# Layer norms over the feature axis: one centring product, squared and scaled straight out of its PSUM bank

## The chip, the cores and the metric

The kernel runs on one core of one Trainium2 chip. The metric is the device time of one execution in microseconds. The core has a matrix engine (TensorE, PE), a vector engine (VectorE, DVE), an activation engine (ScalarE, ACT), a general engine (GpSimd, POOL) and a queue for transfers (SyncE, SP). Each runs its own list of instructions in order and waits on semaphores where it needs another's result. PSUM is the memory that TensorE writes: here banks of 128 x 512 fp32, named pa, pb, ta, tb, c0, c1 and the double bank sc.

## What is computed

Four layers over 4 batches of 1024 tokens with 128 features, each followed by a layer norm of input plus output:

```python
def _layernorm(x, axis=-1, eps=1e-05):
    m = jnp.mean(x, axis=axis, keepdims=True)
    v = jnp.var(x, axis=axis, keepdims=True)
    return (x - m) / jnp.sqrt(v + eps)
...
x = _layernorm(x + _L0_attn_ref(...))   # linear attention with rotations
x = _layernorm(x + _L0_ffn_ref(...))    # two transformer layers, windows of 64
x = _layernorm(x + _L1_attn_ref(...))   # deformable gather of 33 rows a token
x = _layernorm(x + _L1_ffn_ref(...))    # 8 experts, top-2 gating over tokens
```

Each of the two transformer layers has one more norm in front of its feed-forward, with gain and bias:

```python
h = (h - mu) / jnp.sqrt(var + 1e-05) * lg + lb
h = h @ w1 + b1
```

The change is in the norms of the first two layers only. The last two are normed over tokens in another way and stay.

## The kernel before

Activations lie with features on the 128 partitions and 512 tokens (a half, j = 0 or 1) along the free axis. A mean over features is therefore a product with `meanw`, a 128 x 128 matrix filled with 1/128: every partition of the bank then holds the mean of its token.

A batch has eight such norms, m = 0 to 7. Norms 0 and 1 (halves 0 and 1) follow the linear attention. Norms 2 and 3 stand in front of the feed-forward of the first transformer layer, 4 and 5 in front of the second, and their result `hn` feeds the product with `w1`. Norms 6 and 7 follow the second transformer layer and write `x2`. They run in the order 0, 1, 2, 3, 4, 6, 5, 7 (`NORMS`). Over 4 batches that makes 32 norms.

A norm is two steps, `mean` and `var`, in the program of each engine:

- `mean`: TensorE multiplies `meanw` by the source (L1479). VectorE waits for the bank, subtracts it from the source into `lnc` and gives the bank back (L1118). ScalarE waits for that and squares `lnc` into `lnq` (L839).
- `var`: TensorE multiplies `meanw` by the squares (L1484). ScalarE takes Ln out of the bank (L844) and Exp(-0.5 x) in SBUF (L846). VectorE multiplies `lnc` by the result: for norms 0 and 1 into `x1` (L1123), for 2 to 5 with the gain into `lnc` (L1125), for 6 and 7 into `x2`, a part of `xm` (L1131). For norms 2 to 5 ScalarE then adds the bias and writes `hn` (L849), which the first products of the feed-forward read (L1539).

The banks. The products of projections, norms and feed-forward share pa and pb in turn. The function `plan` goes through TensorE's steps in their order and gives every result the next of the two. A product waits (`wait_free`) until the former user of its bank has been drained. So behind `mean m` in one bank and `var m` in the other, the next result takes the bank of `mean m`: behind norm 0 that is `ao 1`, the output product of the attention's second half (L1466), behind norm 1 the query projection of the first tile (L1491), behind norms 2, 3 and 4 a value projection `v` (L1491), behind norm 5 a product of the feed-forward, behind norm 6 the transposes `x2t 0` of its own result, behind norm 7 the second group of transposes of the next batch (L1372).

The order. The steps have due times in tables (`AT`, `first_times`, `late_times`), and each engine's list is sorted by them once, when the program is built. Batch 0 runs alone. Then a loop of three passes computes batch b in its first part (attention and the two transformer layers) beside the second part of batch b - 1, the gather: GpSimd issues indirect transfers of the rows (L744, three for a chunk, 88 chunks for a batch), VectorE weights a chunk (L1240), TensorE sums its transposes (L1591). A ring of 5 chunk buffers couples them. A tail does the second part of batch 3 and the experts. GpSimd also multiplies the weights of each tile of tokens (L759). On VectorE the weighting of a chunk stands between `mean 7` and `var 7`. On ScalarE, in front of the square of norms 2 and 4, stand the exponentials of the softmax (L881) and two copies (L796).

## Time and profile before

| | us |
|---|---|
| time, median of 3 runs | 2317.84 |
| lowest and highest | 2312.19, 2323.54 |
| the profiled execution, its own time | 2323.0 |
| its span, first to last instruction | 2321.0 |
| TensorE busy | 1669.0 (72%) |
| VectorE busy | 1307.1 (56%) |
| GpSimd busy | 1140.6 (49%) |
| ScalarE busy | 969.2 (42%) |

The mean granted clock of TensorE over the span was 0.853 of full speed. The page lists busy time by engine, and then groups of instructions by their line in the program: how often, how long, and for what the engine waited before. The timeline gives single instructions: start, duration, engine, line, "written<-read" tiles, and in square brackets how long the engine had been idle and whose end released it. A row without brackets had its engine busy until then. Matmuls overlap: the row that follows another on TensorE can begin before its end. An fp32 product of 128 x 512 counts as two instructions.

### The profile page before, as it was taken

What the parts mean: (1) busy time and instruction counts of PE and PEld (TensorE: products, weight loads), DVE (VectorE), ACT (ScalarE), POOL (GpSimd) and SP (SyncE); (2) the same over time, 40 slices, a digit from 0 to 9 for tenths busy, and PEclk for the clock granted to TensorE, in tenths of its full rate; (3) what the DMA queues carried; (4) which work ended last, traced back from release to release, by engine and by line L of the source; (5) the groups of instructions that cost most, each with busy time, mean ns of one, the idle gap of its engine ahead of it and who ended that gap; (6) DMA issues with size and microseconds to landing.
All of it is one profiled execution on the core that took longest, in us unless ns stands there. A gap on an engine that the chain in (4) does not pass through costs nothing.

```text
span 2321.0 us, 34040 instructions
## 1 busy us (share of the span) xinstructions
PE 1669.0 (72%) x11753; PEld 1075.6 (46%) x11753; DVE 1307.1 (56%) x2182; ACT 969.2 (42%) x2341; POOL 1140.6 (49%) x1136
## 2 busy tenths in 40 slices
PE   5667675766687767756878758667777567999967
PEld 3343333434454534435545424355445335766747
DVE  6664643567766734667577436576666344343333
ACT  3355553323445553225444623145455333343431
POOL 0000003467766516477676062776763265777710
PEclk8899997878898978779899978788998778999975
DMA  3000003223333323133333231333333252333311
GB/s 126 10 19 14 14 15 64 64 82 110 114 90 90 94 42 89 50 101 112 98 103 101 42 76 43 101 110 101 101 94 73 46 152 67 103 102 102 102 23 37
DMA packets 92404, 178.45 MB, mean 77 GB/s; under 512 B 21434, under 2 KB 49220, under 8 KB 91972
## 3 DMA queue, kind: packets, MB, share of 16 engines
q0 software_dynamic: 50688, 138.48, 21.4%
q1 hardware_dynamic: 41540, 37.70, 5.8%
q8 instruction: 101, 1.65, 0.3%
q14 instruction: 75, 0.61, 0.1%
HBM read 150.93 MB, written 8.92 MB: 69 GB/s over the span
## 4 chain that ended last, share of the span: by engine, by line
PE 33%; DVE 22%; POOL 15%; issue 14%; ACT 11%; DMA 4%; DVEq 0%; POOLq 0%; SPq 0%; ACTq 0%
POOL pool_c L744 14%; PE c L1591 4%; DVE pool_c L1240 4%; DMA pool_c<-rows_of_x,idx 4%; ACT prob L881 3%; DVE ssq L1144 3%; DVE nmax L1154 2%; PE pb L1491 2%; PE pa L1491 2%; DVE pool_a L1197 2%; PE tb L1372 2%; PE pb L1539 2%; PE pa L1539 2%; PE sc L1656 2%; PE pa L1529 1%
## 5 line engine op out<-in xcount | busy, mean ns | idle before, releaser
L744 POOL DMA_INDIRECT pool_c<-rows_of_x,idx x1056 | 1074.9, 1018 | 1070.7 <-issue 655.9
L1240 DVE TENSOR_TENSOR pool_c<-pool_c 128x768 f32<-128x768 f32 x352 | 341.0, 974 | 307.3 <-DMA pool_c<-rows_of_x,idx 268.5
L1591 PE MATMUL c<-ident,pool_c 128*128 128x128 f32 x2112 | 338.1, 305 | 171.3 <-DVE pool_c L1240 171.1
L1591 PEld LDWEIGHTS c<-ident,pool_c 128*128 128x128 f32 x2112 | 278.8, 158 | 298.9 <-DVE pool_c L1240 211.2
L881 ACT ACTIVATE prob<-sc,nmax 128x128 f32<-128x128 f32 x512 | 180.3, 379 | 126.9 <-DVE nmax L1154 126.8
L796 ACT COPY pool_a<-tb 128x512 f32<-128x512 f32 x188 | 112.1, 596 | 69.6 <-PE tb L1372 69.6
L1491 PE MATMUL pa<-wqkv,pool_a 128*128 128x512 f32 x192 | 115.7, 688 | 16.1 <-DVE pool_a L1197 6.9
L1491 PE MATMUL pb<-wqkv,pool_a 128*128 128x512 f32 x192 | 116.4, 693 | 13.3 <-DVE pool_a L1010 6.4
L1521 PE MATMUL ta<-vmix,pool_a 128*64 128x64 f32 x1024 | 79.0, 236 | 62.0 <-ACT pool_a L796 60.1
L881 ACT ACTIVATION_READ_ACCUMULATOR prob<-sc,nmax 128x1 f32 x512 | 111.4, 218 | 0.0
L1144 DVE TENSOR_REDUCE ssq<-pool_a 128x16 f32<-128x1024 f32 x64 | 77.7, 1214 | 57.8 <-ACT pool_a L857 57.7
L1372 PE MATMUL ta<-ident,pool_a 128*128 128x128 f32 x288 | 54.3, 319 | 75.6 <-DVE pool_a L1167 71.6
L1521 PEld LDWEIGHTS ta<-vmix,pool_a 128*64 128x64 f32 x1024 | 71.1, 149 | 75.2 <-issue 74.8
L1372 PE MATMUL tb<-ident,pool_a 128*128 128x128 f32 x544 | 96.0, 305 | 12.1 <-ACT pool_a L796 10.2
L1372 PEld LDWEIGHTS tb<-ident,pool_a 128*128 128x128 f32 x544 | 70.5, 156 | 61.0 <-issue 51.1
L1539 PE MATMUL pa<-pool_a,w 128*128 128x512 f32 (+1 forms) x96 | 68.1, 800 | 32.6 <-ACT pool_a L849 17.7
L857 ACT ACTIVATE pool_a<-pa 128x512 f32<-128x512 f32 x64 | 38.4, 600 | 117.7 <-PE pa L1491 117.7
L863 ACT ACTIVATE ssq<-ssq 128x16 f32<-128x16 f32 x64 | 13.8, 216 | 175.8 <-DVE ssq L1146 175.8
L1154 DVE TENSOR_REDUCE nmax<-sc 128x8 f32<-128x1024 f32 x64 | 77.9, 1217 | 12.8 <-PE sc L1566 12.8
L1214 DVE TENSOR_TENSOR pool_a<-pool_a 128x1024 f32<-128x1024 f32 x64 | 80.4, 1256 | 5.9
L1206 DVE TENSOR_TENSOR pool_a<-pool_a,rot 128x512 f32<-128x512 f32 x128 | 82.7, 687 | 0.1
L1372 PEld LDWEIGHTS ta<-ident,pool_a 128*128 128x128 f32 x288 | 37.0, 161 | 95.5 <-DVE pool_a L1167 84.1
(404 smaller groups left out, 3354.9 us busy)
## 6 DMA issues: line engine op xcount, KB each, us to landing
pool_c<-rows_of_x,idx POOLq DMA_INDIRECT x1056
vmix<-vring SPq DMA_DIRECT2D x128, 128.0 KB
rows_of_x<-x2tok SPq DMA_DIRECT2D x16, 256.0 KB
xtok<-in_x SPq DMA_DIRECT2D x4, 512.0 KB, 4.4
x_of_all<-x2tok SPq DMA_DIRECT2D x8, 256.0 KB, 2.4
out<-pool_c SPq DMA_DIRECT2D x8, 256.0 KB, 2.6
wqkv<-in_wqkv SPq DMA_DIRECT2D x1, 1536.0 KB
xtok<-x_of_all SPq DMA_DIRECT2D x3, 512.0 KB, 6.3
```

The costliest lines, as they stand in the source:

```text
L744: pool.indirect_dma_start(gat[:, n % GB, s, :], None, table, bass.IndirectOffsetOnAxis(ap=idx[:, t, SC * c + s:SC * c + s + 1], axis=0),). ...
L796: nc.scalar.copy(dst, src[:, :] if view is None else view(src)).then_inc(empty(key), 1)
L881: ins = nc.scalar.activation(prob[:, n % 2, pr, e, :], sc[:, e, P * pr:P * (pr + 1)], ACT.Exp, bias=nmax[:, n % 2, e, pr:pr + 1], accum_ou ...
L1144: V.tensor_reduce(ssq[:, t % 2, 0, :], sq[:, :, :].rearrange("p w (h d) -> p (w h) d", h=HB), AXX, ALU.add).then_inc(SEM["b_ss"], 1)
L1154: V.tensor_reduce(nmax[:, n % 2], sc[:, :, :].rearrange("p e (r k) -> p e r k", r=PAIRS), AXX, ALU.max, negate=True).then_inc(SEM["b_max"], 1)
L1206: V.tensor_tensor(r2[:, :, :, at:at + 32], qn[:, :, :, o:o + 32], ap3(rot[:, l, t, 1, 0, at:], [[DH, 2], [0, HB], [1, 32]]), ALU.mult).the ...
L1240: V.tensor_tensor(g4, g4, wv, ALU.mult).then_inc(SEM["c_prod"], 1)
L1372: ins = PE.transpose(out[:, P * i:P * (i + 1)], src(i), ident[:])
L1491: mm(out[:, :], hT[:, P * n:P * (n + 1)], wqkv[:, l, c:c + INNER], start=True, stop=True).then_inc(full(key), 1)
L1521: ins = mm(out[q, DH * (2 * pr + e):DH * (2 * pr + e + 1)], PT[:, n % 2, pr, e, q], v[:, 2 * pr + e, :], start=True, stop=True, skip_group ...
L1539: mm(out[0:w, :], w1[:, l, c:c + w], hn[:, :], start=True, stop=True).then_inc(full(key), 1)
L1591: ins = mm(out[:, c:c + P], x, ident[:], start=(i == 0 and k == 0), stop=(i == BCH - 1 and k == len(parts) - 1), is_transpose=True, skip_g ...
```

## The change

`centre` is a new matrix, the identity less 1/128, made on VectorE once at the start (one instruction of 128 x 128). The first product of a norm uses it in place of `meanw`, so that the bank holds source minus mean. VectorE's subtraction (L1118) is gone. ScalarE squares out of the bank into `lnq`, VectorE scales out of the bank in step `var`, and only that gives the bank back. The semaphore `ln_out` is gone: who waited for it waits for the bank to be drained. The tables of due times and the plan of banks are the same, so every result keeps its bank and its turn.

```diff
+            V.tensor_scalar(centre[:], ident[:], 1.0 / D, None, ALU.subtract)
...
                 elif what == "mean":
                     m, = a
-                    wait_drained(act, ("mean", m), b)
-                    nc.scalar.activation(lnq[:, m % 2, :], lnc[:, m % 2, :], ACT.Square).then_inc(SEM["ln_square"], 1)
+                    src = wait_filled(act, ("mean", m), b)
+                    nc.scalar.activation(lnq[:, m % 2, :], src[:, :], ACT.Square).then_inc(SEM["ln_square"], 1)
...
                     if 2 <= m < 6:
-                        wait(act, "ln_out", b, nth(m) + 1)
+                        wait_drained(act, ("mean", m), b)
...
-                        wait(dve, "f_shift", b, 2 * (m - 2) + 2 + (m == 5))
-                        src = h2[:, :]
-                    elif m >= 6:
-                        wait(dve, "f_res", b, m - 5)
-                    mean = wait_filled(dve, ("mean", m), b)
-                    V.tensor_tensor(lnc[:, m % 2, :], src, mean[:, :], ALU.subtract).then_inc(empty(("mean", m)), 1)
                 elif what == "var":
                     m, = a
                     wait(dve, "ln_rstd", b, nth(m) + 1)
+                    mean = wait_filled(dve, ("mean", m), b)
                     if m < 2:
-                        V.tensor_tensor(block_of(x1, m), lnc[:, m % 2, :], lnq[:, m % 2, :], ALU.mult).then_inc(SEM["ln_out"], 1)
+                        V.tensor_tensor(block_of(x1, m), mean[:, :], lnq[:, m % 2, :], ALU.mult).then_inc(empty(("mean", m)), 1)
                     elif m < 6:
-                        V.scalar_tensor_tensor(lnc[:, m % 2, :], lnc[:, m % 2, :], col(LG + m // 2 - 1), lnq[:, m % 2, :], ALU.mult, ALU.mult).then_inc(SEM["ln_out"], 1)
+                        V.scalar_tensor_tensor(lnc[:, m % 2, :], mean[:, :], col(LG + m // 2 - 1), lnq[:, m % 2, :], ALU.mult, ALU.mult).then_inc(empty(("mean", m)), 1)
...
-                        V.tensor_tensor(x2[:, BLK * (m - 6):BLK * (m - 5)], lnc[:, m % 2, :], lnq[:, m % 2, :], ALU.mult).then_inc(SEM["ln_out"], 1)
+                        V.tensor_tensor(x2[:, BLK * (m - 6):BLK * (m - 5)], mean[:, :], lnq[:, m % 2, :], ALU.mult).then_inc(empty(("mean", m)), 1)
...
-                    mm(out[:, :], meanw[:], src, start=True, stop=True).then_inc(full(("mean", m)), 1)
+                    mm(out[:, :], centre[:], src, start=True, stop=True).then_inc(full(("mean", m)), 1)
...
-                    wait(pe, "ln_out", b, nth(6 + j) + 1)
+                    wait_drained(pe, ("mean", 6 + j), b)
```

On VectorE, in the opening of batch 0, the list holds before the change (`pb` in the second row is the bank of `mean 0`, in the fifth that of `ao 1`, the output product of the attention):

```order
50 L1118 TENSOR_TENSOR lnc<-x,pb 128x512
51 L1084 TENSOR_TENSOR lnc<-sc,lnq 128x512
52 L1090 TENSOR_TENSOR lnc<-lnc,xtok 128x512
53 L1123 TENSOR_TENSOR x<-lnc,lnq 128x512
54 L1094 SCALAR_TENSOR_TENSOR x<-pb,cols,xb 128x512
55 L1118 TENSOR_TENSOR lnc<-x,pa 128x512
```

and after it:

```order
51 L1086 TENSOR_TENSOR lnc<-sc,lnq 128x512
52 L1092 TENSOR_TENSOR lnc<-lnc,xtok 128x512
53 L1119 TENSOR_TENSOR x<-pb,lnq 128x512
54 L1096 SCALAR_TENSOR_TENSOR x<-pb,cols,xb 128x512
55 L1011 COPY pool_a<-x 64x512
```

The subtractions are gone and nothing else changed places: the scaling (53 in both) now reads pb, and the row behind it reads what TensorE writes into the same pb afterwards.

On TensorE, at norm 2 of batch 0, the rows after the change are these (before it they are the same but for `meanw` in the first): `centre` is the first product of the norm, the next is the second, then come the value projection, the transposes `oT`, and the first two products of the feed-forward.

```order
254 L1475 MATMUL pb<-pool_a,centre 128x512
255 L1480 MATMUL pa<-lnq,meanw 128x512
256 L1487 MATMUL pb<-wqkv,pool_a 128x512
257 L1368 MATMUL tb<-ident,pool_a 128x128 x4
258 L1535 MATMUL pa<-pool_a,w 128x512
259 L1535 MATMUL pb<-pool_a,w 128x512
```

Row 256 takes the bank of row 254: nothing moved, but its wait for pb is now a wait for the scaling and no longer for the subtraction.

## Rows read from the trace of the kernel before

**Rows 1.** The page, part 4: chain of work that ended last, share by engine.

```profile
PE 33%; DVE 22%; POOL 15%; issue 14%; ACT 11%; DMA 4%; DVEq 0%; POOLq 0%; SPq 0%; ACTq 0%
```

**Rows 2.** Groups by line: ScalarE's squares, count, busy time and mean ns, idle before them.

```profile
L839 ACT ACTIVATE lnq<-lnc 128x512 f32<-128x512 f32 x32 | 20.4, 639 | 88.1 <-DVE lnc L1118 88.0
```

**Rows 3.** Timeline, batch 0, norms 0 and 1: start us, us, engine, line.

```profile
70.50 0.63 ACT L835 ACTIVATE lnq<-lnq 128x512 f32<-128x512 f32 x1
70.96 0.69 DVE L1118 TENSOR_TENSOR lnc<-x,pb 128x512 f32<-128x512 f32 x1 [1.28 <-PE pb L1479]
...
73.32 1.02 PE L1466 MATMUL pb<-lnc,ow 128*128 128x512 f32 x2
...
74.91 0.69 DVE L1123 TENSOR_TENSOR x<-lnc,lnq 128x512 f32<-128x512 f32 x1 [1.93 <-ACT lnq L846]
...
76.41 1.10 PE L1479 MATMUL pa<-x,meanw 128*128 128x512 f32 x2 [2.06 <-DVE x L1094]
...
79.91 1.02 PE L1491 MATMUL pa<-wqkv,pool_a 128*128 128x512 f32 x2
...
81.49 0.69 DVE L1123 TENSOR_TENSOR x<-lnc,lnq 128x512 f32<-128x512 f32 x1 [2.48 <-ACT lnq L846]
...
83.12 1.22 DVE L1144 TENSOR_REDUCE ssq<-pool_a 128x16 f32<-128x1024 f32 x1
```

**Rows 4.** Timeline, batch 0, norm 2: ScalarE, TensorE and the next bank.

```profile
174.78 0.70 ACT L839 ACTIVATE lnq<-lnc 128x512 f32<-128x512 f32 x1
...
175.53 1.13 PE L1484 MATMUL pa<-lnq,meanw 128*128 128x512 f32 x2 [1.99 <-ACT lnq L839]
...
176.49 1.02 PE L1491 MATMUL pb<-wqkv,pool_a 128*128 128x512 f32 x2
...
178.86 0.72 ACT L849 ACTIVATE pool_a<-lnc,cols 128x512 f32<-128x512 f32 x1 [0.82 <-DVE lnc L1125]
...
180.56 1.28 ACT L901 ACT_TABLE_LOAD   x1
```

**Rows 5.** Timeline, batch 0, norm 4: its second product.

```profile
322.24 2.07 PE L1484 MATMUL pa<-lnq,meanw 128*128 128x512 f32 x2 [1.99 <-ACT lnq L839]
```

**Rows 6.** Timeline, batch 2, norms 0 and 1, while GpSimd gathers.

```profile
966.07 1.12 PE L1466 MATMUL pb<-lnc,ow 128*128 128x512 f32 x2 [0.58 <-DVE lnc L1090]
...
968.27 0.69 DVE L1123 TENSOR_TENSOR x<-lnc,lnq 128x512 f32<-128x512 f32 x1
...
971.64 0.96 DVE L1240 TENSOR_TENSOR pool_c<-pool_c 128x768 f32<-128x768 f32 x1 [2.02 <-DMA pool_c<-rows_of_x,idx]
...
981.28 1.91 PE L1491 MATMUL pa<-wqkv,pool_a 128*128 128x512 f32 x2
```

**Rows 7.** Timeline, batch 2, norm 2: the projection behind the norm, and the scaling.

```profile
1128.84 1.92 PE L1491 MATMUL pb<-wqkv,pool_a 128*128 128x512 f32 x2
1129.19 0.75 DVE L1125 SCALAR_TENSOR_TENSOR lnc<-lnc,cols,lnq 128x512 f32<-128x512 f32 x1 [4.28 <-ACT lnq L846]
```

**Rows 8.** Timeline, end of batch 2's pass, norm 7.

```profile
1379.68 1.02 PE L1479 MATMUL pb<-xb,meanw 128*128 128x512 f32 x2
...
1386.98 0.96 DVE L1240 TENSOR_TENSOR pool_c<-pool_c 128x768 f32<-128x768 f32 x1 [2.29 <-DMA pool_c<-rows_of_x,idx]
1387.34 2.77 PE L1591 MATMUL c<-ident,pool_c 128*128 128x128 f32 x12
...
1388.97 2.01 DVE L1131 TENSOR_TENSOR xm<-lnc,lnq 128x512 f32<-128x512 f32 x1 [1.02 <-ACT lnq L846]
```

**Rows 9.** Timeline, batch 1, norm 2 beside GpSimd's own multiply.

```profile
636.11 0.69 DVE L1118 TENSOR_TENSOR lnc<-pool_a,pb 128x512 f32<-128x512 f32 x1 [1.29 <-PE pb L1479]
636.21 1.54 POOL L759 TENSOR_TENSOR pool_c<-pool_c 128x264 f32<-128x264 f32 x2
```

**Rows 10.** Timeline, batch 3, norm 7 and the transposes that wait for it.

```profile
1877.09 1.96 DVE L1131 TENSOR_TENSOR xm<-lnc,lnq 128x512 f32<-128x512 f32 x1 [1.14 <-ACT lnq L846]
...
1879.10 0.66 PE L1372 MATMUL c<-ident,xm 128*128 128x128 f32 x4 [0.87 <-DVE xm L1131]
```

More of the change, by code:

```diff
@@ L354, in build @@
         meanw = sb("meanw", [P, P])
+        centre = sb("centre", [P, P])
         blockd = sb("blockd", [P, D // G])
@@ L505, in build @@
             "x_loaded": 16, "a_rot": 8, "a_scan": 16, "a_state": 2, "a_zero": 1, "a_att": 1, "a_square": 2, "a_rstd": 2, "a_y": 3,
-            "ln_square": 8, "ln_rstd": 8, "ln_out": 8,
+            "ln_square": 8, "ln_rstd": 8,
             "b_shift": 8, "b_square": 32, "b_ss": 32, "b_rn": 32, "b_cos": 16, "b_sin": 32, "b_qk": 16,
@@ L1096, in first @@
                     m, = a
-                    src = block_of(x1 if m < 2 else xb, m % 2)
                     if 2 <= m < 6:
@@ L1134, in first @@
                     if l == 0:
-                        wait(dve, "ln_out", b, j + 1)
+                        wait_drained(dve, ("mean", j), b)
                     else:
```

## The prediction

> **What bounds the kernel now.** I read first the chain of work that ended last, then the groups by line for the lines that the change touches, and then the timeline around each of the eight norms, in batch 0 and in the passes of the loop, since each has another limit. The chain has no one engine [rows 1]: TensorE 33%, VectorE 22%, GpSimd 15%, ScalarE 11%. The kernel is bound by hand-overs between engines, and a shorter step helps only where that step was the last to arrive. ScalarE's 32 squares waited 88.0 us in all for the subtraction in front of them [rows 2]. That number tempts: a subtraction of 0.69 us with its hand-over is 0.7 us, and 32 of them are 22.4 us. But idle time before a square is not time lost, and the same edit makes the next user of the bank wait for the end of the norm. Both have to be read place by place.
>
> **Batch 0, norms 0 and 1: slower.** Nothing runs beside batch 0. Its first norm [rows 3]: the subtraction begins at 70.96. Without it the square has to wait for ScalarE's own Exp (70.50 + 0.63 = 71.1) and not for 70.96 + 0.69 = 71.65, so the norm is 0.5 us earlier; its scaling begins at 74.4 and not at 74.91, and ends at 75.1. The output product `ao 1` goes into the bank of norm 0. It began at 73.32, under the norm, since the subtraction had given the bank back. Now it begins at 75.1, takes the 1.1 us of a lone product, and VectorE reads it at 76.2 and not at 74.91 + 0.69 = 75.6. Norm 1 thus starts about 0.6 us later than its 76.41. It then saves a whole subtraction (0.7) and scales at 81.4, practically the old 81.49, until 82.1. The query projection, which takes its bank, began at 79.91 and now begins at 82.15; the pair ends two products later (2 x 1.0) at 84.2, the square of the second is 0.6, and the reduction that waits for it begins at 84.8 and not at 83.12: **+1.7 us**.
>
> **Batch 0, norms 2 to 4: slower.** The square of norm 2 at 174.78 has no bracket [rows 4]: ScalarE came to it from its own work, and the subtraction was hidden. No gain. The value projection takes the norm's bank: at 176.49 before, now not before the scaling is over, just ahead of ScalarE's bias step at 178.86. It ends at 180.0, the transposes behind it at 180.5, and ScalarE's two copies (0.5 each: between 178.86 + 0.72 and 180.56 there are two) end at 181.5, where the table for the Gelu is loaded; before that was 180.56: **+1.0 us**. Norm 4 has the same order: **+1.0 us**. Norm 3 has only one copy behind the projection, and two transposes on TensorE stand ahead of its second product. Between nothing and norm 2's 1.0 I take the middle: **+0.5 us**. Norms 5 and 6 come to ScalarE behind its own work too, and their bank goes to someone who needs the result of the norm anyway: 0. Batch 0 together: 1.7 + 1.0 + 0.5 + 1.0 = **+4.2 us**. Making `centre` is one small instruction of VectorE in its first chain: +0.1.
>
> **The passes of the loop, norms 0 and 1: nothing.** There GpSimd's gather sets the pace: VectorE waits for rows to land [rows 6], 2.02 us before the weighting at 971.64. The output product began at 966.07; now it waits for the scaling at 968.27 to end (968.96), ends at 970.1, and VectorE has read it by 970.9, still 0.7 us before the rows land. The scaling itself stands behind the weighting of a chunk, so it is not earlier either. If that cover were gone, each opening would cost 0.6 us as in batch 0. The query projection at 981.28 came after the scaling of norm 1 already. Queued behind the output product on TensorE are sums of chunks; they free buffers of a ring of five, and are late by some 2 us where GpSimd needs them several chunks on.
>
> **The passes, norms 2 to 4: nothing, with a spread.** Here the square did wait for the subtraction. The value projection began at 1128.84 and the scaling at 1129.19 [rows 7]. Without the subtraction the scaling is at 1128.5 and ends at 1129.2, so the projection is 0.4 us later and what hangs on the scaling 0.7 earlier. ScalarE needs both in turn. I take 0 for each of the 9 places. The ends are a whole subtraction gained (-0.7) and the 1.0 lost of batch 0, together -6.3 to +9.
>
> **Norm 7: faster.** Its first product had run at 1379.68 [rows 8], but the subtraction stood on VectorE behind the weighting of a chunk that landed late, and square, second product and the sums behind it followed. Now ScalarE squares at once, and the second product is done before the next weighting (1386.98 + 0.96 = 1387.94). The pass ends on TensorE with the sums of that chunk: the last half of the pair that took 2.77 from 1387.34 to 1390.11, so 1387.95 + 1.4 = 1389.3, or 1388.8 at the faster rate. I take -1.0 at the end of batches 1 and 2: **-2.0 us**. The end of batch 0 lies under GpSimd's gathers: 0. In batch 3 the transposes of x2 wait for the scaling [rows 10]: it began at 1877.09, 1.14 after the weighting ahead of it, and took 1.96. Now it begins at 1875.95. TensorE has one chunk's sums to do first (0.9 to 1.4), so the transposes start near 1877.1 and not at 1879.10: **-2.0 us**.
>
> **How long the scaling takes.** Beside GpSimd's multiply, the scaling of norm 7, both inputs in SBUF, took 2.01 and 1.96 us [rows 8, 10]; the subtraction of norm 2, one input in PSUM, took 0.69 us with that multiply started 0.1 us after it [rows 9]. I use 0.7 us for the scaling out of the bank in all places. The Trainium skill, "SBUF — State Buffer", section "Who interferes with whom", says that a VectorE instruction with two SBUF inputs contends with a GpSimd instruction that reads SBUF, and one with at most one SBUF input does not. By it four scalings would be 1.3 us shorter; the sum is the same without it, since the new scaling begins ahead of the multiply.
>
> **The clock.** Norm 2's second product followed a pause of 1.99 us and took 1.13 [rows 4]; norm 4's followed the same pause and took 2.07 [rows 5]. So products run at either of two levels after equal pauses, and one product at the lower level costs 0.94. The held bank stretches five pauses of TensorE in batch 0 beyond 2 us, and the missing subtraction shortens others. I take one product at the lower level more, rounded to +0.7. The Trainium skill, "TensorE: Matmul & The Clock Gate", section "HAM oscillation — how this bites in real kernels", describes a kernel whose waits let the clock drop again and again. It speaks against a change that makes TensorE wait for a bank, and is rival C.
>
> **The sum.** 4.2 + 0.1 - 2.0 - 2.0 + 0.7 = +1.0 us. The profiled execution was 2323.0 us with a span of 2321.0, so 2324.0; against the median of 2317.84 the same sum gives **2318.8 us**. TensorE, VectorE and ScalarE are less busy or the same, and no transfer changes.
>
> **Rivals.**
> A, faster: the 88.0 us were mostly on the chain. Then each of 32 norms is 0.7 us shorter and the longer hold is hidden: 2317.8 - 22.4 = 2295.4. For it: the squares did wait, and VectorE loses 32 instructions. Against it: rows 3, 4 and 6, where the next user of the bank, ScalarE's own work or a landing comes last. It decides if over half of the squares outside batch 0 are on the chain.
> B, slower: the held bank costs in every batch what it costs in batch 0, and norm 7 gives nothing: 4 x 4.2 = 16.8, 2334.6. Its place is the projection behind norms 0 to 4; it decides where the 0.7 us of cover before the landing [rows 6] and the 0.7 of the scaling [rows 7] are used up.
> C, slower by the clock: all five held products of all four batches run at the lower level: 20 x 0.94 = 18.8, 2336.6. Against it: in the passes chunk sums stand between.
>
> **How the numbers follow.** Forecast 0.68, A 0.17, B 0.10, C 0.05. The forecast's own spread is -6.3 to +9 around 2318.8, thus 2312 to 2328, and the runs shown scatter by 5 us either way. The range 2307 to 2332 takes that in and some of the partial forms of A and B, and leaves about 2 in 10 out. Within 0.5% (11.6 us) is about what a measurement of this kernel can tell from no change. Faster by more is A in its fuller forms, 0.18 with the edge of the forecast; slower is B and C, 0.15; the same is 0.67.
>
> **What would show it.** In batch 0 the reduction behind norm 1 at 84.8 (before 83.12) and the table load behind norm 2 about 2.7 us after its old time; the first gather of GpSimd some 4 us later. In the passes the output product of norm 0 directly behind the scaling, with VectorE still waiting for the landing after it. At norm 7 the square more than 3 us earlier and the scaling 0.7 us long directly behind the weighting. The forecast is wrong if the first gather is not later, or if the length of the second and third pass changes by more than 3 us.

## The result: slower by 13 us, outside the forecast

| | us |
|---|---|
| before, median of 6 runs (lowest, highest) | 2321.6 (2312.2, 2323.9) |
| after, median of 6 runs (lowest, highest) | 2334.7 (2331.6, 2340.6) |
| after / before | 1.0064, 95% interval 1.0043 to 1.0086 |
| profiled execution after: span | 2333.1 (before 2321.0) |
| forecast | 2318.8, range 2307 to 2332 |

The change costs 13.1 us by medians and 14.9 by means (0.64%; the interval of 0.43% to 0.86% is 10 to 20 us). TensorE's instructions are the same but for the matrix in the first product of a norm, yet the page gives it 1680.2 us busy where it gave 1669.0; VectorE has 26.7 us less. The chain has moved from VectorE and GpSimd to TensorE [rows 1] (the page, part 4, after):

```profile
PE 36%; DVE 21%; issue 13%; POOL 13%; ACT 12%; DMA 4%; DVEq 0%; POOLq 0%; SPq 0%; ACTq 0%
```

ScalarE's wait ahead of the squares, the tempting 88.0 us [rows 2], is now a wait for the product, and did not vanish: 33.6 us for one bank here and 28.3 us for the other, together 61.9.

```profile
L840 ACT ACTIVATE lnq<-pb 128x512 f32<-128x512 f32 x16 | 9.7, 605 | 33.6 <-PE pb L1475 33.6
```

**Where the time went.** The first product of norm 0 in batch 0 starts 1.1 us earlier than before, and GpSimd's first gather 15.2 us later (393.29, was 378.12). From there to the end of the span the two profiles differ by 3.1 us in favour of the changed kernel. The windows view of TensorE, from each first product of a norm to the next (norms 0, 1, 2, 3, 4, 6, then the first gather; columns: window, its length, TensorE busy, instructions, granted clock, DMA share, GB/s). Before:

```profile
69.82:76.41 6.59, 3.08 (x7) 1.00 0.00 0
76.41:172.41 96.00, 62.83 (x532) 0.93 0.08 17
172.41:236.40 63.99, 42.32 (x302) 0.89 0.06 13
236.40:319.12 82.72, 58.42 (x494) 0.96 0.08 17
319.12:352.20 33.08, 25.43 (x191) 0.85 0.07 16
352.20:378.12 25.92, 16.15 (x80) 0.90 0.15 41
```

After:

```profile
68.73:76.39 7.66, 3.71 (x6) 0.88 0.00 0
76.39:177.12 100.73, 66.91 (x532) 0.86 0.07 17
177.12:245.68 68.56, 45.67 (x302) 0.85 0.06 12
245.68:331.03 85.35, 61.32 (x495) 0.92 0.07 16
331.03:367.51 36.48, 27.66 (x190) 0.77 0.07 15
367.51:393.29 25.78, 17.00 (x80) 0.84 0.15 42
```

The same products (a few records differ in number): 308.3 us long with 208.2 busy before, 324.6 with 222.3 after. 14.0 of the 16.3 us are TensorE being busy longer, and the granted clock has fallen in every stretch.

**What happens at a held product.** A product is called held here when it has to wait for the scaling because its bank is kept until then. Batch 0, norms 0 and 1, after (timeline; answers to rows 3):

```profile
73.12 0.69 DVE L1119 TENSOR_TENSOR x<-pb,lnq 128x512 f32<-128x512 f32 x1 [1.56 <-ACT lnq L847]
73.96 1.49 PE L1462 MATMUL pb<-lnc,ow 128*128 128x512 f32 x2 [2.26 <-DVE x L1119]
...
76.39 2.04 PE L1475 MATMUL pa<-x,centre 128*128 128x512 f32 x2 [0.94 <-DVE x L1096]
...
79.12 2.07 PE L1480 MATMUL pb<-lnq,meanw 128*128 128x512 f32 x2 [0.69 <-ACT lnq L840]
...
83.45 2.04 PE L1487 MATMUL pa<-wqkv,pool_a 128*128 128x512 f32 x2 [2.26 <-DVE x L1119]
...
85.28 1.91 PE L1487 MATMUL pb<-wqkv,pool_a 128*128 128x512 f32 x2
...
87.87 1.22 DVE L1140 TENSOR_REDUCE ssq<-pool_a 128x16 f32<-128x1024 f32 x1 [3.66 <-ACT pool_a L858]
```

`ao 1` stands directly behind the scaling, as forecast. But in front of it TensorE was idle for 2.26 us, where before the product had filled this time, and what follows runs at the lower of its two levels (1.2 instead of 2.4 GHz): not one product, but nearly all work to 87 us. The granted clock over 74.0 to 87.2 us is 0.52; before it was 1.00 over the same work (69.8 to 83.1 us). From norm 0's first product to the reduction it was 13.30 us before and is 19.14. Norm 2 (answers to rows 4) shows the same, down to the transposes:

```profile
180.21 1.97 PE L1480 MATMUL pa<-lnq,meanw 128*128 128x512 f32 x2 [1.96 <-ACT lnq L840]
...
184.38 0.72 ACT L850 ACTIVATE pool_a<-lnc,cols 128x512 f32<-128x512 f32 x1 [0.82 <-DVE lnc L1121]
184.50 2.05 PE L1487 MATMUL pb<-wqkv,pool_a 128*128 128x512 f32 x2 [2.32 <-DVE lnc L1121]
...
186.34 1.06 PE L1368 MATMUL tb<-ident,pool_a 128*128 128x128 f32 x4
...
187.19 1.92 PE L1535 MATMUL pa<-pool_a,w 128*128 128x512 f32 x2
...
188.58 1.28 ACT L902 ACT_TABLE_LOAD   x1
```

Norm 4 (rows 5) likewise: its value projection took 2.04 us after a pause of 2.32.

### The profile page after: what moved, and what is told of

Its sections match the earlier page's. It is cut to its first block, busy times and chain, and to the rows that moved or that the text cites. A ratio compares the mean times of both kernels' runs of the same rounds, so it can differ in the third digit from the quotient of the medians.

```text
span 2333.1 us, 33988 instructions
## 1 busy us (share of the span) xinstructions
PE 1680.2 (72%) x11745; PEld 1081.7 (46%) x11753; DVE 1280.4 (55%) x2151; ACT 970.2 (42%) x2341; POOL 1137.4 (49%) x1136
## 4 chain that ended last, share of the span: by engine, by line
PE 36%; DVE 21%; issue 13%; POOL 13%; ACT 12%; DMA 4%; DVEq 0%; POOLq 0%; SPq 0%; ACTq 0%
POOL pool_c L745 12%; PE c L1587 4%; DMA pool_c<-rows_of_x,idx 3%; DVE pool_c L1236 3%; PE pa L1487 3%; ACT prob L882 3%; DVE ssq L1140 3%; PE pb L1487 2%; DVE nmax L1150 2%; PE tb L1368 2%; PE pb L1535 2%; DVE pool_a L1193 2%; PE pa L1535 2%; PE sc L1652 1%; PE ta L1368 1%
## 5 line engine op out<-in xcount | busy, mean ns | idle before, releaser
L1487 PE MATMUL pa<-wqkv,pool_a 128*128 128x512 f32 x192 | 121.6, 720 | 23.3 <-DVE lnc L1121 7.0
L1487 PE MATMUL pb<-wqkv,pool_a 128*128 128x512 f32 x192 | 118.6, 704 | 27.1 <-DVE lnc L1121 11.5
L1368 PE MATMUL tb<-ident,pool_a 128*128 128x128 f32 x544 | 99.0, 312 | 12.1 <-ACT pool_a L797 10.2
L1205 DVE TENSOR_TENSOR pool_a<-pool_a,rot 128x1024 f32<-128x1024 f32 x64 | 83.3, 1301 | 2.2
```

The costliest lines, as they stand in the source:

```text
L1205: V.tensor_tensor(qn, qn, ap3(rot[:, l, t, 0, 0, :], [[DH, 2], [0, HB], [1, DH]]), ALU.mult).then_inc(SEM["b_cos"], 1)
L1368: ins = PE.transpose(out[:, P * i:P * (i + 1)], src(i), ident[:])
L1487: mm(out[:, :], hT[:, P * n:P * (n + 1)], wqkv[:, l, c:c + INNER], start=True, stop=True).then_inc(full(key), 1)
```

## The experiments

Theory H: the longer hold is the cause, and most of its price is the clock of the products behind the stretched pause. Its rivals: D, something else in the change; the hold's waits alone, without the clock. On the place there are two theories: B0, the loss arises in batch 0; PA, it arises in the passes. On the pause there are two: S, the pause of the hold is what matters; E, the pause ahead of the norm's second product counts alike.

Each row of the table is one profile. Lengths of batch 0 in the profiles, in us (a norm 2, 3 or 4 is measured from its first product to ScalarE's table load):

| kernel | norm 0 to reduction | norms 2, 3, 4 | norm 0 to first gather |
|---|---|---|---|
| before | 13.3 | 8.2, 8.1, 9.1 | 308.3 |
| before_again | 15.2 | 8.9, 8.1, 9.1 | 312.2 |
| changed (after) | 19.1 | 11.5, 9.3, 11.6 | 324.6 |
| after_again | 18.9 | 10.6, 9.5, 10.8 | 318.6 |
| hold_alone | 20.7 | 10.6, 9.7, 11.3 | 322.7 |
| wait_in_batch0 | 20.6 | 10.6, 9.7, 11.4 | 323.7 |
| wait_in_batch0b | 20.2 | 11.5, 9.7, 11.3 | 323.1 |
| fill_hold_only | 15.2 | 10.2, 9.5, 9.3 | 315.3 |
| fill_square_only | 18.9 | 10.6, 11.7, 10.6 | 321.6 |
| fill_pauses | 15.3 | 9.3, 11.7, 9.2 | 317.4 |
| old_and_fill | 15.1 | 8.5, 9.1, 8.5 | 313.4 |
| turn_bank | 11.9 | 7.8, 9.5, 8.5 | 313.2 |
| turn_but_norm3 | 11.8 | 7.8, 9.1, 7.8 | 311.9 |

Seven more profiles (late_norms_new, the four runs of the wait in the passes, the two of new_in_passes) have the old norms 0 to 4 in batch 0, and took 311.6 to 315.3. With before and before_again the nine give a mean of 313.1; the five that hold and fill nothing (changed, after_again, hold_alone, wait_in_batch0, wait_in_batch0b) give 322.5, and their lowest, 318.6, lies above the highest of the nine. So the first profile of before was the luckiest of nine, and the hold costs 9.4 us in batch 0, not the 16.3 that one pair of profiles shows.

**hold_alone: the hold without the rest.** The old norm, but the subtraction signals by a semaphore of its own, and the scaling gives the bank back. Against the kernel before it comes down to this:

```diff
-V.tensor_tensor(lnc[:, m % 2, :], src, mean[:, :], ALU.subtract).then_inc(empty(("mean", m)), 1)
+V.tensor_tensor(lnc[:, m % 2, :], src, mean[:, :], ALU.subtract).then_inc(SEM["ln_sub"], 1)
...
-... lnq[:, m % 2, :], ALU.mult).then_inc(SEM["ln_out"], 1)
+... lnq[:, m % 2, :], ALU.mult).then_inc(empty(("mean", m)), 1)
```

> The old norm (mean by meanw, subtraction on VectorE into lnc, square and scaling from lnc), with one difference: the bank of the mean is given back only by the scaling, as in the changed kernel. So only the longer hold is left of the change. Theory H (the longer hold is the cause: the projection behind a norm waits for the scaling, and the stretched pause of TensorE is followed by products at the lower clock): batch 0 is as late as in the changed kernel or later, first gather of GpSimd near 393 to 396 us where before had 378.1, and the whole near 2335 to 2342. Theory D (the cause lies in what else changed: the squares and scalings out of PSUM, or the missing work of VectorE, which shifts when everything behind starts): first gather near 378 to 381, the whole within 4 us of before, 2318 to 2326.

Measured: 1.0077 (1.0048 to 1.0105), median 2339.7 beside 2322.2. (Here and below: time by that of the kernel before, measured beside it, with the 95% interval.) First gather 392.3. The hold alone costs as much as the change or more; D falls.

**turn_bank: the change without most of the hold.**

```diff
-    "mean": lambda m: [(("mean", m), PROJ)],
+    "mean": lambda m: [(("mean", m), TURN if m in (0, 1, 2, 4) else PROJ)],
```

> The changed kernel, but the centring products of norms 0, 1, 2 and 4 go into the banks ta and tb, which the transposes use, so that the next product finds pa or pb free while the norm runs. The subtraction stays away, the hold hurts nobody but the transposes. Theory H: batch 0 gets back what it lost but for norm 3, and gains the missing subtraction at norms 0 and 1 (0.5 + 0.7): first gather 376 to 381, the whole 2312 to 2322. If the hold cost only its waits and the clock fell for another reason, the first gather stays at 388 or later and the whole at 2330 or more. Theory A (a subtraction that is on the chain nearly everywhere, hidden so far by the hold): 2298 to 2306.

Measured: 1.0000 (0.9977 to 1.0022), first gather 383.3. The loss is gone, as H says. The first gather is 2 us behind the 376 to 381 that H named; that range had been reckoned from the 378.1 of the first profile. Rival A falls too: with the hold nearly gone, 32 missing subtractions give nothing that can be measured in the whole. They do show in place, 11.9 us at norms 0 and 1 where the nine old profiles have 13.3 to 15.2. Norm 3, still held, takes 9.5 where they have 8.1 to 9.1.

**fill_pauses: the hold with a busy TensorE.** In batch 0, products of `ident` by `ident` are added, into banks that are overwritten next: five in the pause ahead of a norm's second product, eight in the pause of the hold. Norm 3 has only the first five.

```diff
-                    wait(pe, "ln_square", b, nth(m) + 1)
                     out = wait_free(pe, ("var", m), b)
+                    if at_start(b):
+                        for _ in range(5):
+                            mm(out[:, 0:P], ident[:], ident[:], start=True, stop=True)
+                    wait(pe, "ln_square", b, nth(m) + 1)
                     mm(out[:, :], meanw[:], lnq[:, m % 2, :], start=True, stop=True).then_inc(full(("var", m)), 1)
+                    nxt = {0: ("qT", 0, 0), 1: ("qT", 0, 0), 2: ("oT", 0, 4), 3: None, 4: ("oT", 1, 4)}.get(m)
+                    if at_start(b) and nxt is not None:
+                        out = wait_free(pe, nxt, b)
+                        for _ in range(8):
+                            mm(out[:, 0:P], ident[:], ident[:], start=True, stop=True)
```

> The changed kernel with products added in batch 0 alone, whose results are overwritten before anything reads them: 5 of 128x128 ahead of each second product of a norm, while TensorE waits for the square, and 8 behind it, into the bank of a transpose that comes next, while it waits for the held bank. Waits and hold stay as in the changed kernel, only TensorE is no longer idle in them. If most of the 15 us that batch 0 lost are products at the lower clock (theory H with the clock as its larger part: 13.2 us more busy time for the same products): granted clock of 70 to 180 us back to 0.93 or more, first gather 380 to 386, the whole 2320 to 2328. If the waits themselves are the 15 us: first gather at 393 or later, the whole 2334 to 2340.

Measured: 1.0012 (0.9990 to 1.0034), median 2326.6; 1.0064 without the fill. The norms 0 and 1 take 15.3 us instead of 19.1 with the same waits, norm 2 9.25 instead of 11.46. The granted clock of 70 to 180 us is 0.91, where 0.93 or more was expected. At norm 3 the added products came in the way of the norm's own second product, which starts 5.7 us behind the first instead of 3.3 (11.7).

**late_norms_new: the change only where nobody is held** (norms 5, 6, 7; 0 to 4 in the old form).

> The new form only for norms 5, 6 and 7, whose bank nobody waits for who doesn't need the norm's result anyway; norms 0 to 4 in the old form. Theory H: no product is held, batch 0 as before (first gather 378 to 379), and norm 7 gives what the prediction said, 1 us in two passes and 2 at the end of the third: 2315 to 2320, 2 to 5 us below before. If norm 7's gain is taken back by the next wait, 2320 to 2323. Theory D: slower than before in part, 2325 or more.

Measured: 0.9992 (0.9971 to 1.0013), median 2320.8. No loss; the gain of 2 to 5 us isn't shown. Its first gather came at 384.3, where 378 to 379 was expected, with norms 0 to 4 that are those of before. So one profile of the old form doesn't tell the length of batch 0.

**Long passes.** Beside every run from here to new_in_passes, the kernel before itself took 2531 to 2566 us and not 2322. Batch 0 is as long as elsewhere. The passes are not: in the profiles of before and before_again, from norm 0 of one batch to that of the next, the second pass took 484 and 548 us, the third 488 and 561, and the rest behind it 872 and 967. That is more than the 30 us for a pass that some of the expectations below name. Of these runs only the ratios, each against the kernel before beside it, and the lengths of batch 0 are used. The chain of before_again has an entry that the page of before lacks:

```profile
PE 33%; DVE 19%; issue 16%; another core or an unknown queue 11%; ACT 10%; POOL 9%; DMA 2%; DVEq 0%; SPq 0%; POOLq 0%; ACTq 0%
```

All twelve profiles with long passes have this entry, and none of the eight others. In before_again GpSimd waits 54 times, 108.6 us in all, between its gathers for what the profile puts down to another core or an unknown queue. What that is stays open.

**wait_in_batch0, wait_in_passes: the hold as a bare wait.** Before, with one wait added on TensorE:

```diff
             reach(eng, drained[bank], (b + (bank in CB)) * turns[bank] + n)
+            if n:
+                last = next((k for k, v in where.items() if v == (bank, n - 1)), None)
+                if last and last[0] == "mean" and last[1] in (0, 1, 2, 3, 4) and at_start(b):
+                    wait(eng, "ln_out", b, nth(last[1]) + 1)
             return psum[bank]
```

`last` is the former user of the bank. In wait_in_passes and its repeats the condition ends in `not at_start(b)`.

> The kernel before with one thing added, in batch 0 alone: the product that takes the bank of norms 0 to 4 (ao 1, a query projection, three value projections) also waits for the scaling of that norm. No instruction is added, left out or moved. Theory B0 (the loss arises in batch 0, where nothing else fills TensorE, and is carried to the end): first gather of GpSimd 8 to 15 us later than in the kernel before, the whole 2330 to 2338. Theory PA (the 12 to 15 us of batch 0 in one profile were mostly the clock's scatter, and the loss is made in the passes): first gather within 5 us, the whole 2320 to 2327.

Measured: 1.0044 (1.0017 to 1.0071), 7.8 us more by medians and 11.7 by means. First gather 392.2, where before_again has 381.5. Not an instruction differs from before but that wait. Norm 2 there:

```profile
185.17 2.05 PE L1495 MATMUL pb<-wqkv,pool_a 128*128 128x512 f32 x2 [2.32 <-DVE lnc L1129]
```

> The same added wait, but in the three passes of the loop and not in batch 0. Theory B0: chunk sums and landings cover it, as the prediction held: the whole 2319 to 2326. Theory PA: the whole 2330 to 2338, and the passes together 8 to 15 us longer than in the kernel before. Between the two, a share of the loss in each: 2326 to 2330 here and about as much there.

Measured: 0.9999 (0.9967 to 1.0032). With long passes the wait cost nothing there.

> The kernel before, with the products of the run fill_pauses added in the same places of batch 0 (5 of 128x128 ahead of the second product of a norm, 8 behind it, overwritten before anything reads them). It is the control of that run, which was 8 us below the changed kernel. If filled pauses help because the hold had stretched them, they do little here: 2319 to 2324. If they help in any kernel, since the clock of batch 0 is held up: 2312 to 2318, and then only the difference between this run and fill_pauses is the price of the hold itself.

Measured: 1.0006 (0.9979 to 1.0034), batch 0 of 313.4 us, the mean of the old form. Filled pauses are no gain of their own; what fill_pauses gave back was the hold's. The 4.0 us between this batch 0 and that of fill_pauses are the hold with its pauses filled.

> The kernel before, unchanged, to see how far one profiled execution of it stands from another, stage by stage. If the length of batch 0 is the same in each execution, the first gather is at 378 and every norm within 1 us of the first profile; if TensorE's clock makes it scatter, as the run late_norms_new suggests (its norms 0 to 4 are those of before, and its first gather came at 384.3), it lies anywhere between 376 and 386, and the length of the whole stays in 2313 to 2331.

Measured: 1.0011 (0.9973 to 1.0048), batch 0 3.9 us longer than in the first profile: TensorE's clock scatters. Norm 2's second product took 1.13 us in the one and 1.89 in the other after pauses of 1.99 and 1.98.

**fill_hold_only, fill_square_only: which pause it is.** The two halves of fill_pauses.

> The changed kernel with only half of the added products of fill_pauses: 8 of 128x128 behind the second product of a norm in batch 0, in the pause that the held bank makes, none ahead of it. Theory S (the pause that the hold stretches to 2.3 us is what lets the clock fall; the pause before the second product was there before and matters little): nearly as good as both fills, first gather 386 to 388 where the changed kernel had 393.3, the whole 5 to 8 us below the changed kernel. Theory E (both pauses count alike): first gather 389 to 391, the whole about 4 us below it.

> The changed kernel with the other half: 5 products of 128x128 ahead of each second product of a norm in batch 0, in the pause in which TensorE waits for the square, none behind it. Theory S: the clock still falls in the hold, first gather 390 to 393, the whole 0 to 3 us below the changed kernel. Theory E: as the other half, first gather 389 to 391, about 4 us below.

Measured against before: 1.0068 (1.0037 to 1.0100) and 1.0096 (1.0063 to 1.0130); batch 0 315.3 and 321.6 us, first gather 383.9 and 390.5. The products of the hold's pause give back 7.2 us on the mean of the five held profiles, those of the square's pause 0.9, or some 3 if the 2.4 us by which they delay norm 3's second product are added. So batch 0 speaks for theory S. The wholes don't: the changed kernel was not measured beside them, and both stand above the kernel before with intervals that overlap. The loss of fill_hold_only in the whole must lie mostly behind batch 0, in the long passes. In fill_hold_only, norms 0 and 1 (timeline):

```profile
71.43 1.95 PE L1521 MATMUL ta<-ident 128*128 128x128 f32 x16
...
73.86 1.10 PE L1495 MATMUL pb<-lnc,ow 128*128 128x512 f32 x2 [0.47 <-DVE x L1152]
...
81.12 1.10 PE L1528 MATMUL pa<-wqkv,pool_a 128*128 128x512 f32 x2 [0.48 <-DVE x L1152]
...
83.74 1.22 DVE L1173 TENSOR_REDUCE ssq<-pool_a 128x16 f32<-128x1024 f32 x1 [1.86 <-ACT pool_a L877]
```

The products wait for the scaling as in the changed kernel, but run 1.10 us and not 1.49 and 2.04.

> Again the added wait of norms 0 to 4 in the three passes and not in batch 0, since in the call of wait_in_passes the passes of every kernel were some 30 us longer than usual, with rows landing later, and a wait is covered more easily there. If the cover is there at the usual length too, the whole is within 3 us of the kernel before; if it was only the late rows that covered it, 5 to 12 us above.

Measured: 1.0069 (1.0040 to 1.0097), where the same kernel had 0.9999. Not settled by these two.

> As turn_bank, but norm 3, whose projection was still held there, in the old form: no product is held anywhere, and all other norms go without the subtraction. In turn_bank the stages behind norms 0, 1, 2 and 4 of batch 0 were 0.7 to 1.7 us shorter than with the old form and that behind norm 3 2.3 to 5 us longer. If stages add up: first gather 376 to 380, the whole 2 to 6 us below the kernel before. If the passes take nothing from the missing subtraction and the clock eats the rest: within 2 us of it.

Measured: 1.0042 (1.0012 to 1.0072), both expectations missed. Batch 0 is 311.9 us, 1.2 less than in turn_bank, and the first gather came at 382.5 instead of 376 to 380; the whole is slower where it should be faster. With the long passes even the form that holds nothing lost 10 us, and this stays unexplained.

> The changed kernel itself, beside the other three of this call, to see how firm its batch 0 is from one execution to the next. Theory B0: first gather again at 391 to 394 and the whole 10 to 15 us above the kernel before. If the first profile showed an unlucky clock: first gather at 386 or less, the whole 0 to 7 us above.

Measured: 1.0108 (1.0076 to 1.0139), +24 us by medians; batch 0 at 318.6 us, 6 less than in the first profile and still above all old ones. The first gather, 387.4, lies between the two expectations: part of the 324.6 of the first profile was an unlucky clock.

> Again the kernel before with the wait for the scaling added in batch 0 alone, hoped for on a chip where the passes have their usual length. Theory B0: first gather near 392, the whole 10 to 13 us above the kernel before, as much as the changed kernel or 2 us less. Theory PA: 3 to 6 us above.

Measured: 1.0047 (1.0021 to 1.0073), +8.1 us by medians, between the two theories; the first gather, 391.7, is where B0 put it.

> Again the wait in the passes alone, whose two runs before contradict each other (0 and 15 us above the kernel before, both with passes 30 us longer than usual). Theory B0: 0 to 3 us above the kernel before where the passes have their usual length. Theory PA: 7 to 12 us above.

Measured: 1.0051 (1.0029 to 1.0072), +11.6 us by medians, as PA says.

> The changed form in the passes and the old form for norms 0 to 4 of batch 0, where nothing covers the held bank. Theory B0: no loss in batch 0 (first gather 378 to 384), and the gain at norm 7 that the prediction held is all that is left: 2 to 5 us below the kernel before. If the passes give nothing from the missing subtraction: within 2 us of it. Theory PA: 5 to 10 us above.

```diff
+        def form(m, b):
+            return "old" if m in OUTN and at_start(b) else "new"
```

`OUTN` is (0, 1, 2, 3, 4). Measured: 1.0080 (1.0052 to 1.0107), +22 us by medians: more than either theory named. With long passes most of the loss lies in them.

The two runs that follow had passes of the usual length (before: 2325.7 us).

> The wait in the passes alone, once more. Three calls gave 0, +15 and +12 us beside the kernel before, all with passes about 30 us longer than in the kernel's usual runs. If this call has passes of usual length: Theory B0 says 0 to 3 us above the kernel before, Theory PA 7 to 12 us. If its passes are long again, only the mean of four such calls follows, and the question stays open for the usual length.

Measured: 1.0032 (1.0016 to 1.0048), +5.6 us by medians and +7.6 by means: between the two theories.

> Old form for norms 0 to 4 in batch 0, changed form in the passes, once more. At passes of usual length: Theory B0 says 2 to 5 us below the kernel before; if hold and missing subtraction cancel in the passes, within 2 us; Theory PA 5 to 10 us above. With long passes it was 20 us above.

Measured: 1.0007 (0.9989 to 1.0024), 1.6 us less by medians. So in passes of the usual length the held bank costs about 7 us (hold_alone, 16.4 us by means with 9.6 of them in batch 0, says the same), and the missing subtraction gives back about as much, give or take 4.

The profiles say so less clearly. From first product to table load, the nine norms 2 to 4 in the passes sum to these, at the usual length:

| form in the passes | us |
|---|---|
| old (before, late_norms_new) | 79.9, 80.6 |
| old and held (hold_alone, wait_in_passes4) | 89.7, 87.9 |
| changed (after, fill_pauses, new_in_passes2) | 84.2, 89.4, 79.7 |

How a gain can come about shows at norm 2 of batch 2. Before (the first row is the norm's second product; rows 7 have the next ones):

```profile
1125.70 2.07 PE L1484 MATMUL pa<-lnq,meanw 128*128 128x512 f32 x2 [1.51 <-ACT lnq L839]
```

wait_in_passes4:

```profile
1136.98 2.07 PE L1488 MATMUL pa<-lnq,meanw 128*128 128x512 f32 x2 [1.52 <-ACT lnq L843]
...
1141.37 2.04 PE L1495 MATMUL pb<-wqkv,pool_a 128*128 128x512 f32 x2 [1.04 <-DVE lnc L1129]
```

new_in_passes2:

```profile
1128.03 1.12 PE L1516 MATMUL pa<-lnq,meanw 128*128 128x512 f32 x2 [0.76 <-ACT lnq L862]
...
1131.48 1.13 PE L1523 MATMUL pb<-wqkv,pool_a 128*128 128x512 f32 x2 [1.67 <-DVE lnc L1157]
```

Without the subtraction the pause ahead of the second product is 0.76 and not 1.51 us, and both products ran at the upper level. It need not be so: norm 2 of the three batches took 8.1 us each time in new_in_passes2, and 11.0, 11.1 and 8.1 in the changed kernel, which has the same form there.

## Why the prediction was wrong, point by point

- **The 88.0 us are not on the chain:** right. turn_bank lacks all 32 subtractions and holds hardly anything, and stands at 1.0000. Rival A is out.
- **Norms 0 and 1 of batch 0, +1.7:** the place, the order and the wait were right, the size was not. The reduction was to start at 84.8 and started at 87.9. The mean of the two profiles of the changed kernel is 19.0 us, that of the nine old ones 14.4: +4.7. With the hold's pause filled it is 15.2, which is +0.8.
- **Norms 2, 3 and 4, +1.0, +0.5, +1.0:** by the same means +2.1, +1.1 and +2.1. Again the wait was right and what follows it missing.
- **The waits together, +4.2:** near in sum, and not place by place. With all pauses filled, the hold costs 4.0 us in batch 0 (fill_pauses beside old_and_fill), but of its norms 0 and 1 have 0.2, norms 2 and 4 have 0.7 each and norm 3 has 2.6. That the sums agree is partly luck.
- **The clock, +0.7: the step that failed.** It priced one product more at the lower level. The rows used for it (norm 2 and norm 4 after equal pauses of 1.99) told that such a pause may or may not cost; they said nothing of one that is 2.3 us long and comes soon after another. In the five profiles that hold and fill nothing the value projection behind norms 2, 3 and 4 took 2.04 or 2.05 us in 14 of 15 cases (1.10 in the other). In the changed kernel the four transposes and the next two products behind it ran at that level too, wholly or in part, at norms 2 and 4 (1.06 us, then 1.92 and 1.87, or 1.91 and 1.66), and one product in part at norm 3 (1.68). The term should have been 5 to 7 us: 9.4 less the 4.2 of the waits is 5.2, and filling the hold's pause gave back 7.2. The Trainium skill, "TensorE: Matmul & The Clock Gate", section "HAM oscillation — how this bites in real kernels", tells of a kernel in which each wait lets the clock drop anew; the trace of batch 0 agrees in kind, with a granted clock of 0.77 where it was 0.85 behind norm 4, though its waits are of 2.3 us and those of that kernel were for transfers and longer. It had been weighed as rival C at 0.05, priced there for all four batches at one product each. The form that came true was in one batch, with several products each.
- **The passes, norms 0 and 1, nothing:** right. From norm 0's first product to the reduction it is 26.6, 26.7 and 24.6 us, before 26.2, 27.0 and 26.8. The output product stands behind the scaling, and VectorE still waits 0.28 us for the rows, where 0.7 was forecast (answers to rows 6):

```profile
990.62 0.69 DVE L1119 TENSOR_TENSOR x<-pb,lnq 128x512 f32<-128x512 f32 x1
991.36 1.12 PE L1462 MATMUL pb<-lnc,ow 128*128 128x512 f32 x2 [3.43 <-DVE x L1119]
...
993.55 0.96 DVE L1236 TENSOR_TENSOR pool_c<-pool_c 128x768 f32<-128x768 f32 x1 [0.28 <-DMA pool_c<-rows_of_x,idx]
```

- **The passes, norms 2 to 4, nothing with a spread of -6.3 to +9:** not refuted. By the whole times (new_in_passes2) the passes lose nothing that can be measured, as a balance of two larger effects; the changed kernel's own profile has +4.3 for the nine norms, within the spread. The clock decides more here than the 0.4 us that were weighed: the shortest such stretch is 7.7 us in the old form and 8.1 in the new, and norm 2 in the new form took up to 11.1.
- **Norm 7, -2.0 at the ends of batches 1 and 2, -2.0 in batch 3: the second step that failed.** The norm did get shorter, but the stage behind it did not. The end of batch 2's pass, after (answers to rows 8):

```profile
1405.68 0.96 DVE L1236 TENSOR_TENSOR pool_c<-pool_c 128x768 f32<-128x768 f32 x1 [2.76 <-DMA pool_c<-rows_of_x,idx]
1406.55 0.68 DVE L1127 TENSOR_TENSOR xm<-pb,lnq 128x512 f32<-128x512 f32 x1
1406.69 1.54 PE L1587 MATMUL c<-ident,pool_c 128*128 128x128 f32 x6 [2.84 <-DVE pool_c L1236]
...
1410.81 1.11 PE L1368 MATMUL pa<-ident,xtok 128*128 128x128 f32 x4 [2.58 <-issue]
```

The scaling is 0.68 us long as forecast and starts 8.15 us behind the norm's first product instead of 9.29, the last sums end 9.8 instead of 10.4 behind it, and the next pass begins 12.41 instead of 12.16 behind it. The profile calls the pause in front of it "issue", 2.58 us where it was 1.73; its cause is open. In batch 3 the transposes do start 1.75 us earlier (answers to rows 10):

```profile
1887.83 0.69 DVE L1127 TENSOR_TENSOR xm<-pb,lnq 128x512 f32<-128x512 f32 x1
...
1888.90 1.55 POOL L760 TENSOR_TENSOR pool_c<-pool_c 128x264 f32<-128x264 f32 x2
...
1889.30 1.06 PE L1368 MATMUL c<-ident,xm 128*128 128x128 f32 x4
```

But they prepare the gather of the second half, and GpSimd, which had begun the first at 1847.9, was still at it until 1905 without a pause, so from norm 7 to the last gather it is 345.8 us after and 345.3 before. So the -2.0 of batch 3 had no waiting consumer behind it, and of the -2.0 at the ends of batches 1 and 2 the next pass shows nothing. The whole of late_norms_new, 1.5 us less by medians with an interval of -6.7 to +3.0, neither shows the -4.0 nor excludes it.
- **The scaling out of the bank at 0.7 us:** right (0.68 and 0.69). In none of the profiles did a scaling out of a bank run beside GpSimd's multiply, so its price there is untested; with both inputs in SBUF and no multiply beside it, it took 0.69 us too (wait_in_passes4, norm 7 of batch 2).
- **The sign named beforehand:** the forecast was to be wrong if the second or third pass changed by more than 3 us. From norm 0 to norm 0 they took 484.2 and 488.0 us and take 491.0 and 485.9, so it came true for the second. But late_norms_new, with the old norms 0 to 4, has 484.2 and 481.9: 3 us is less than such lengths scatter.

Together, in the usual passes: batch 0 +9.4 where +5.0 stood (4.2, 0.1 and the clock's 0.7), passes and tail +1.7 by the ratio of new_in_passes2 (-2.6 to +5.6) where -4.0 stood. That makes +11; measured were 13.1 and 14.9, with an interval from +10. Of the 12 to 14 us that the forecast was short, 4.5 are the clock behind the held products of batch 0 and 4.0 are norm 7; the other 4 to 5 are not placed. Rivals B and C named times near the right one (2334.6, 2336.6) with the loss in all four batches; it lies mostly in the first.

**What stays open:** what makes the passes long in some measurements; why then the added wait in them cost 0, 15 and 12 us; and why there even turn_but_norm3, which holds nothing, was slower. One profile each, with stages that scatter by some 7 us, doesn't settle it. At the usual length it is open how the 4 to 5 us behind batch 0 come about. No version was found that beats the kernel before; late_norms_new and turn_bank equal it.

## What to carry to other kernels

Before a bank is held longer, look at what its next user did for TensorE: a product that ran under a dependency chain also kept the clock up, and its delay is paid by the products behind it too. Price such a pause with everything that runs after it until the engine is busy again, and test it with products whose result nobody reads. A step made shorter is a gain only with the name of who waited for it; norm 7 had none.

## What the runs showed of the hardware

- The same 128 x 512 fp32 product took 1.10 us after a pause of 0.53 us and 2.04 us after a pause of 2.32 us, at the same place of the program (fill_hold_only, shown here, and the changed kernel, norm 4 of batch 0):

```profile
331.68 1.10 PE L1528 MATMUL pb<-wqkv,pool_a 128*128 128x512 f32 x2 [0.53 <-DVE lnc L1154]
```

- Batch 0 up to the first gather took 308.3 to 315.3 us in nine profiles with the same norms 0 to 4, and the granted clock went with it (the stretch between norms 1 and 2: 96.0 us at 0.93, 99.3 at 0.85). One pair of profiles can't price a change of 10 us here.
- The kernel before took 2322 to 2326 us in some measurements and 2531 to 2566 us in others. It is not the chip alone: chip 2 gave both 2531 and 2326. The difference lies in the passes and the gather behind them, not in batch 0. GpSimd's indirect transfers took 1.018 us each to issue in both, but it stood idle 1071 us between them in before and 1314 in before_again.
